# Weighted sums, the turned input and the normalisation in other slots of a four-slot attention step

## The reference, cut to what matters

```
h   = norm(x); h = windows(roll(h))            # layer 0: over the image; layers 1 to 3: over each token
q, k, v = split(h @ qkv_w + qkv_b)             # 12 heads of 8 in layers 0 to 2, 4 heads of 24 in layer 3
attn = softmax(q * scale @ k.T + rel_bias + mask)
x   = x + unwindow(attn @ v @ proj_w + proj_b)
x   = x + mlp(norm(x))                         # 96 -> 384 -> 96, GELU between
```

## Time and profile before

| | |
|---|---|
| runs | 8190.55, 8194.28, 8196.19 us |
| profiled execution | 8198.08 us, span of its instructions 8196.3 us |
| mean granted TensorE clock | 0.992 of full speed |
| TensorE matmul busy | 7699.8 us, 94% |
| VectorE busy | 6095.8 us, 74% |
| ScalarE busy | 4936.6 us, 60% |
| GpSimd busy | 5289.4 us, 65% |
| DMA, mean rate | 28 GB/s |

### The profile page before, as it was taken

The page is one execution under the profiler, slowest core; times in us unless marked ns, Lnnn a source line. Parts: engine busy times, 40 slices in busy tenths (PEclk is TensorE's granted clock), DMA queues, the critical chain, the costliest instruction groups (busy, mean ns, idle before and its releaser), DMA issues.

```text
span 8196.3 us, 312040 instructions
## 1 busy us (share of the span) xinstructions
PE 7699.8 (94%) x109686; PEld 5836.7 (71%) x109686; DVE 6095.8 (74%) x18297; ACT 4936.6 (60%) x8745; POOL 5289.4 (65%) x6553
## 2 busy tenths in 40 slices
PE   5999999999899999999989999999999999999998
PEld 3677777767667777776767777777776677777777
DVE  6777778767777777876777677776687778778677
ACT  3746647557674765745767475574576647566457
POOL 4856656556785665656778465564678856566566
PEclk9999999999999999999999999999999999999999
DMA  1101101010010110101011011010101101011010
GB/s 60 37 11 28 50 13 31 11 33 17 24 37 30 32 46 17 31 7 39 11 30 37 30 32 41 21 31 7 40 5 34 56 10 30 14 25 29 11 39 24
DMA packets 309909, 227.60 MB, mean 28 GB/s; under 512 B 217379, under 2 KB 305766, under 8 KB 306344
## 3 DMA queue, kind: packets, MB, share of 16 engines
q1 hardware_dynamic: 307858, 215.98, 9.8%
q10 hardware_dynamic: 1622, 6.13, 0.2%
HBM read 117.62 MB, written 104.37 MB: 27 GB/s over the span
## 4 chain that ended last, share of the span: by engine, by line
PE 68%; DVE 14%; issue 9%; DVEq 3%; ACT 3%; POOL 2%; POOLq 0%; ACTq 0%; DMA 0%; SPq 0%
PE ps L932 11%; PE ps L992 11%; PE ps L893 8%; PE ps L1035 7%; PE ps L1008 7%; PE ps L917 7%; PE ps L939 5%; PE ps L962 3%; PE ps L972 3%; DVE bst L1061 3%; DVE S L1259 2%; PE ps L981 2%; ACT PT L797 2%; DVE xn L1210 2%; PE ps L1022 2%
## 5 line engine op out<-in xcount | busy, mean ns | idle before, releaser
L657 POOL TENSOR_TENSOR S<-S,mx 113x588 f32<-113x588 f32 (+1 forms) x2048 | 2065.8, 1009 | 1369.6 <-DVE mx L1261 1368.2
L797 ACT ACTIVATE PT<-ps 123x490 f32<-123x490 f32 (+1 forms) x2048 | 1061.5, 518 | 1088.3 <-PE ps L992 1082.5
L1259 DVE TENSOR_TENSOR S<-ps,bias 113x588 f32<-113x588 f32 (+1 forms) x1536 | 959.2, 624 | 744.5 <-PE ps L917 743.6
L1261 DVE TENSOR_REDUCE mx<-S 113x12 f32<-113x588 f32 (+1 forms) x2048 | 1359.9, 664 | 71.0
L780 ACT ACTIVATE S<-S 113x588 f32<-113x588 f32 (+1 forms) x2048 | 1249.2, 610 | 269.3 <-POOL S L657 257.8
L992 PEld LDWEIGHTS ps<-turn,S 113*123 113x123 f32 (+2 forms) x8704 | 965.6, 162 | 493.7 <-issue 304.2
L992 PE MATMUL ps<-turn,S 113*123 113x113 f32 (+2 forms) x8704 | 1270.4, 271 | 8.4 <-ACT S L780 6.2
L1008 PEld LDWEIGHTS ps<-w,G 128*98 128x98 f32 x12288 | 1150.4, 167 | 159.3 <-issue 87.5
L932 PEld LDWEIGHTS ps<-Va,PT 123*49 123x49 f32 (+1 forms) x18432 | 825.2, 125 | 497.4 <-issue 403.5
L1008 PE MATMUL ps<-w,G 128*98 128x96 f32 (+1 forms) x12288 | 1151.3, 250 | 0.0
L932 PE MATMUL ps<-Va,PT 123*49 123x27 f32 (+1 forms) x18432 | 984.8, 207 | 166.3 <-ACT PT L797 98.5
(11 more groups left out here) (94 smaller groups left out, 12002.7 us busy)
## 6 DMA issues: line engine op xcount, KB each, us to landing
v_between<-Vd SPq DMA_DIRECT2D x384, 165.4 KB
Va<-v_between SPq DMA_DIRECT2D x768, 41.3 KB
Vb<-v_between SPq DMA_DIRECT2D x768, 27.6 KB
v_between<-Vd SPq DMA_DIRECT2D x128, 153.1 KB
Vl<-v_between SPq DMA_DIRECT2D x256, 76.6 KB
out_dram<-x SPq DMA_DIRECT2D x15, 1176.0 KB
x<-x_dram SPq DMA_DIRECT2D x14, 1176.0 KB
mask<-mask_dram SPq DMA_DIRECT2D x258, 37.5 KB
```

Source lines behind the costliest of these rows:

```text
L657: pool.tensor_tensor(v, v, m, ALU.subtract).then_inc(a_sub, 1)
L797: act.activation(PT[0:rows, (s + 3) % 4, 0:blocks, :].rearrange("p b q -> p (b q)"), ps[0:rows, PT_BANK, 0:blocks * PAIR], ACT.Copy).then_ ...
L1259: dve.tensor_tensor(dst, scores, b, ALU.add).then_inc(a_bi, 1)
L1261: dve.reduce_max(mx[:, e, 0:nh], S[:, e, 0:n].rearrange("p (h k) -> p h k", k=N), axis=AX.X).then_inc(a_mx, 1)
```

## The change

On TensorE the turned input of quad i + 2 (981) is issued in slot 3 directly after the scores, ahead of the weighted sums. On ScalarE its copy `hT` (802) stands in slot 3 ahead of the copy of the transposed `Ot`; the first key copy stands in slot 0 after the exponential, no longer at the head of slot 1; the second key copy precedes the query copy. On GpSimd both normalisation instructions stand in slot 0, around the subtraction of the maxima, and the copy of the statistics with the power in slot 2, no longer in slot 0. On VectorE the aggregation stands in slot 3, no longer in slot 1. No instruction is added or removed.

```diff
--- before.py
+++ after.py
@@ -650,23 +650,7 @@
                             if early(l, i) and not isinstance(g, int):
                                 pool.wait_ge(m_w2, base - 1)
                             masked(i + 1, j + 1, 0)
-                        if on(0):
-                            wait(a_mx, i.pair(s))
-                            v = S[:, s % 2, 0:n].rearrange("p (h k) -> p h k", k=N)
-                            m = mx[:, s % 2, 0:HEADS[l]].unsqueeze(2).to_broadcast([TOK, HEADS[l], N])
-                            pool.tensor_tensor(v, v, m, ALU.subtract).then_inc(a_sub, 1)
-                        if l == 0 and s == 3 and i.static and i.index == NQ - 1:
-                            image_rstd(g, 1, 0)
-                        if s == 0 and on(-3):
-                            done = i - 3
-                            wait(a_agg, done)
-                            stand(pool)
-                            pool.tensor_copy(mv[:, bass.ds(done.index * QUAD, QUAD), :],
-                                             agg[:, (j + 1) % 2, :, :]).then_inc(a_mv, 1)
-                            if l > 0:
-                                wait(a_mv, done)
-                                token_rstd(Unit(done.index * QUAD, None), 2 * l - 1)
-                        if s == 1 and l > 0 and on(2):
+                        if s == 0 and l > 0 and on(2):
                             ahead = i + 2
                             four = bass.ds(ahead.index * QUAD, QUAD)
                             known = (g * RSTD_PHASES + 2 * l - 2) * NQ + ahead.index + 1
@@ -676,7 +660,23 @@
                             pool.tensor_tensor(xn[:, :, :], x[:, bass.ds(xb + ahead.index * QUAD, QUAD), :],
                                                mv[:, four, 0:1].to_broadcast([PAIR, QUAD, C]),
                                                ALU.subtract).then_inc(a_xc, 1)
-                        if s == 2 and l > 0 and on(2):
+                        if on(0):
+                            wait(a_mx, i.pair(s))
+                            v = S[:, s % 2, 0:n].rearrange("p (h k) -> p h k", k=N)
+                            m = mx[:, s % 2, 0:HEADS[l]].unsqueeze(2).to_broadcast([TOK, HEADS[l], N])
+                            pool.tensor_tensor(v, v, m, ALU.subtract).then_inc(a_sub, 1)
+                        if l == 0 and s == 3 and i.static and i.index == NQ - 1:
+                            image_rstd(g, 1, 0)
+                        if s == 2 and on(-3):
+                            done = i - 3
+                            wait(a_agg, done)
+                            stand(pool)
+                            pool.tensor_copy(mv[:, bass.ds(done.index * QUAD, QUAD), :],
+                                             agg[:, (j + 1) % 2, :, :]).then_inc(a_mv, 1)
+                            if l > 0:
+                                wait(a_mv, done)
+                                token_rstd(Unit(done.index * QUAD, None), 2 * l - 1)
+                        if s == 0 and l > 0 and on(2):
                             wait(a_xc, i + 2)
                             pool.tensor_tensor(xn[:, :, :], xn[:, :, :],
                                                rstd[:, bass.ds((i + 2).index * QUAD, QUAD)].unsqueeze(2)
@@ -768,25 +768,30 @@
                         e = (s + 1) % 2
                         prior = i.pair(s - 1)
                         has_prior = on(-1) if s == 0 else on(0)
-                        if s == 1 and on(1):
+                        if has_prior:
+                            wait(a_sub, prior)
+                            act.activation(S[:, e, 0:nh * N], S[:, e, 0:nh * N], ACT.Exp).then_inc(a_exp, 1)
+                        if s == 0 and on(1):
                             wait(a_k, i + 1)
                             if nh == 12:
                                 key_slot(0)
                             else:
                                 act.activation(Kfull[:, o, :, :].rearrange("p j n -> p (j n)"), keys_at(l, i),
                                                ACT.Copy).then_inc(a_ke, 1)
-                        if has_prior:
-                            wait(a_sub, prior)
-                            act.activation(S[:, e, 0:nh * N], S[:, e, 0:nh * N], ACT.Exp).then_inc(a_exp, 1)
+                        if s == 1 and nh == 12 and on(1):
+                            key_slot(1)
                         if s == 1 and on(1):
                             wait(a_q, i + 1)
                             act.activation(QT[:, o, :, :].rearrange("p j n -> p (j n)"),
                                            queries_at(l, i), ACT.Copy,
                                            scale=float(C // nh) ** -0.5).then_inc(a_qe, 1)
-                        if s == 1 and nh == 12 and on(1):
-                            key_slot(1)
                         if s == 2 and nh == 12 and on(1):
                             key_slot(2).then_inc(a_ke, 1)
+                        if s == 3 and on(2):
+                            wait(a_t1, i + 2)
+                            act.activation(hT[0:C, :, :, :].rearrange("p j w n -> p (j w n)"), turned_at(l, i),
+                                           ACT.Identity, bias=gb[:, l, 1:2],
+                                           scale=gb[:, l, 0:1]).then_inc(a_ht, 1)
                         if s == 3 and on(-1):
                             wait(a_ot, i - 1)
                             act.activation(OT[0:C, :, :].rearrange("p j n -> p (j n)"), OTps,
@@ -797,11 +802,6 @@
                             act.activation(
                                 PT[0:rows, (s + 3) % 4, 0:blocks, :].rearrange("p b q -> p (b q)"),
                                 ps[0:rows, PT_BANK, 0:blocks * PAIR], ACT.Copy).then_inc(a_pte, 1)
-                        if s == 3 and on(2):
-                            wait(a_t1, i + 2)
-                            act.activation(hT[0:C, :, :, :].rearrange("p j w n -> p (j w n)"), turned_at(l, i),
-                                           ACT.Identity, bias=gb[:, l, 1:2],
-                                           scale=gb[:, l, 0:1]).then_inc(a_ht, 1)
 
                 mwait = waits(act)
                 lbase = g * NQ
@@ -916,6 +916,16 @@
                                         keys, out = Kfull[rows, t, s, N * w:N * (w + 1)], Sps4[to, k, :]
                                     last = pe.matmul(out, q, keys, start=True, stop=True)
                             last.then_inc(a_sc, 1)
+                        if s == 3 and on(2):
+                            if early(l, i) and i.index == -1:
+                                busy(4, 1)
+                            wait(a_xn, i + 2)
+                            if on(1) and not early(l, i):
+                                wait(a_ke, i + 1)
+                            for p in range(QUAD):
+                                last = pe.transpose(turned_at(l, i)[:, PAIR * p:PAIR * (p + 1)], xn[:, p, :],
+                                                    ident[0:PAIR, 0:PAIR])
+                            last.then_inc(a_t1, 1)
                         if on(-1) if s < 3 else on(0):
                             wait(a_pte, i.pair(s - 3))
                             p = (s + 1) % 4
@@ -971,16 +981,6 @@
                             for p in range(QUAD):
                                 last = pe.transpose(ps[0:C, Z_BANK, PAIR * p:PAIR * p + TOK], Ot[:, p, :], turn[:, :])
                             last.then_inc(a_ot, 1)
-                        if s == 3 and on(2):
-                            if early(l, i) and i.index == -1:
-                                busy(4, 1)
-                            wait(a_xn, i + 2)
-                            if on(1) and not early(l, i):
-                                wait(a_ke, i + 1)
-                            for p in range(QUAD):
-                                last = pe.transpose(turned_at(l, i)[:, PAIR * p:PAIR * (p + 1)], xn[:, p, :],
-                                                    ident[0:PAIR, 0:PAIR])
-                            last.then_inc(a_t1, 1)
                         if on(-1) if s == 0 else on(0):
                             wait(a_pte, before)
                             if i.static and i.index == 0 and s > 1:
@@ -1286,6 +1286,7 @@
                             if not (i.static and i.index < 4):
                                 wait(a_mv, i - 4)
                             stats(i - 2, xb, (i - 2).index * QUAD, QUAD, t, a_bn)
+                        if s == 3 and on(-2):
                             aggregate(i - 2, QUAD, t, a_bn, a_agg)
                         if l == 0 and i.static and i.index == NQ - 1 and s == 1:
                             image_squares(g, 1, 0)
```

## The result

The changed kernel takes 7911.24 us (median of four runs, 7908.55 to 7914.78) against 8195.24 us, a ratio of 0.9654 with a 95% interval of 0.9638 to 0.9671: 284 us less. The forecast was 7925. The profiled execution took 7913.45 us, at a mean granted clock of 0.991.

What follows compares the result with a forecast made beforehand. TensorE was taken as the bound, idle ahead of slot 3's sums. Gains of 0.75, 0.52, 0.52 and 0.53 us in layers 0 to 3, times 29 x 4, gave 269 us: 8194.3 to 7925 us, range 7850 to 8070.

Steps and rivals of the forecast that it cites:

- The bound: TensorE, idle 0.68, 0.33 and 0.41 us a step in layers 0, 1 and 3, in slot 3 ahead of the sums.
- Ot as the cause: In slot 3, Ot ends TensorE's wait ahead of the sums, though layer 1's row names a copy on ScalarE.
- The turned input ahead of the sums: Slot 3: gains 0.75 us a step in layer 0, 0.40 in layers 1 and 2, 0.48 in layer 3, if Ot is there.
- Ot's rest: Slot 3: wait for Ot left after the move; some 0.1 us on average in layer 0, under 0.05 in layers 1 and 2.
- The aggregation: Leaving slot 1 on VectorE brings bias(2) and Ot 0.13 to 0.2 us sooner; costs nothing in the pause after max(3).
- GpSimd's block: Copy, addition and power leave the way of sub(1), so turns(1) come 0.16 us sooner; 1.73 room ahead of sub(3) for 1.72.
- The slack of exp(3): If sub(3) slips, exp(3) has about 0.6 us to spare before turns(3); layer 3 uses it in part, at no cost.
- The early normalisation: GpSimd slot 0: subtraction of the mean, 0.83 us, goes into the 1.52 us pause ahead of sub(0), costing nothing.
- Slots 0 to 2: Slots 1 and 2 together gain 0.16 us in layers 1 and 2; slot 0 of layer 0 gains about 0.1.
- Ot is not late: Rival 1, chance 0.13: Ot still late in slot 3, half the idle time stays, gain 100 to 130 us, 8080 us.
- GpSimd does not hold up pair 3: Rival 3, chance 0.05: GpSimd's block delays sub(3), and the mean's subtraction sub(0); slower, 8590 us with nothing hidden.
- the aggregation took 0.37 us in its new place: Rival 4, chance 0.03: GpSimd blocks the aggregation in slot 3, +0.7 us a step, 8500 us.

Runs made afterwards that it cites:

- the doubled reciprocals: Reciprocals of slot 2 taken twice, once into an unread tile: kernel before 8590.92 us (ratio 1.0404), changed kernel 7978.16 us (0.9736).
- the run with the statistics back: Changed kernel with GpSimd's statistics and power back in slot 0, ahead of sub(1), normalisation still early: 7958.11 us, ratio 0.9708.
- two runs: Kernel before with only TensorE's new order, 10456.98 us; changed kernel with GpSimd's order of before, 10148.0 us.

## Why the prediction was right, step by step

**The bound.** TensorE's idle time ahead of the sums was what had to be removed. It is gone, and TensorE's share of the chain rose to 80%.

**Ot as the cause.** Shown by the doubled reciprocals: the wait grows with Ot in all layers, and in even steps the sums start 0.28 to 0.29 us after Ot's end in layer 1, in the kernel before and in the five runs above in which they wait for it at the upper level.

**The turned input ahead of the sums.** Forecast 0.65, 0.36 and 0.48 us a step with Ot's rest. Slot 3 gained 0.63 in layer 0, 0.31 in layer 1 and 0.40 in layer 3. Each is a little less, since the sums follow the turned input by 0.14 more than turns(2) had.

**The aggregation.** Right in kind: bias(2) follows the scores and the new place is free. The prediction put it in only as what brings Ot's rest down, and it has no term of its own; taken back alone it costs 112 us.

**GpSimd's block.** Sub(1) 0.16 us sooner was forecast, 0.18 measured, by the run with the statistics back. The room ahead of sub(3) sufficed in layer 1: sub(3) follows the power without a gap. In layer 3, with two instructions more, sub(3) starts at 3653.59, 0.98 after max(3) ended. The slack of exp(3) takes that up, as forecast: slot 0, which has turns(3), lasts 2.35 us as before.

**The early normalisation.** This step failed in part. I gave it "nothing", which is its cost, and did not see that the move of the turned input depends on it. In the earlier trace rows the multiplication ends at 2804.62, and the new place of the turned input is at 2803.34. That row stood there. The forecast was not harmed, as the change has both parts; my expectations of two runs were, by over 2000 us.

**Slots 0 to 2.** Forecast 0.16 in layers 1 and 2 for slots 1 and 2 together; they gained 0.18 (slot 1 gained 0.20, slot 2 lost 0.02). Slot 0 of layer 0 gained 0.19, where 0.10 was put in without a row for it; that is why layer 0 gave 0.82 and not 0.75. In the kernel before this slot took 3.23 us in layer 0 and 3.04 in layer 1, which would have told it. Layer 3 gained 0.11 in slot 2, where 0.05 was put in.

**How much of the nearness is luck.** The sum over the steady steps came out at 269 us, as forecast, because errors offset each other: slot 3 gave 23 us less than was put in, slots 0 to 2 some 23 us more. The 15 us outside the steady steps were left at nothing and stand for the whole distance from 7925.

**The rivals.** Ot is not late, GpSimd does not hold up pair 3, and the aggregation took 0.37 us in its new place. By the rule of the Trainium skill that the prediction cites ("SBUF — State Buffer", section Who interferes with whom) nothing was to be added to bias and Ot beside their new neighbours, and the trace agrees: they take 0.77 and 0.56 us, as before.

## What to carry to other kernels

When an instruction is brought forward to fill a wait, look first at when each of its own inputs is there: the row of the producer tells it. A chain from engine to engine starts at one instruction of the bound engine, and what shortens a slot in the middle of it is given back at its end. Parts of a reordering are not additive: here TensorE's part alone costs 2262 us (some 290 by the late rows, the rest by the clock), the rest alone gives 148, and both give 284.

## What the runs showed of the hardware

The clock's fall was not expected. In the run with TensorE's order alone an idle wait of 1.43 us, in a stretch with TensorE busy for 22.54 of 26 us, was followed by the lower level. Near 680 and 788 us the upper level came back within the pass, and both times it was lost again behind the next wait for xn. It rose again at 1192 us, in the last steps of the pass, and the MLP that follows ran at the upper level.

The kernel before, busy for 21.30 of 22.66 us, never fell in its attention loops, nor did the run with 21.29 of 23.28 in the pass shown, though its steps there have waits of 1.09 and 0.90 us. Yet in the same run a pass of layer 3 fell behind a wait of 0.97 us, and another pass of layer 3 did not fall. What tells these apart, and why the clock stayed down from 800 to 1192 us with TensorE busy all the time, these runs do not show. An idle time that seems small is dear where it tips the clock: at least 1925 us here.
